# Attention probabilities: from TensorE transposes to DMA transposes of 16-bit halves, with the row sums divided out of the weighted heads

## What is computed

```python
x = x + xattn(ctx, layernorm(x), ...)      # 64 sequences, 16 heads of 64
# in xattn, with ln1/ln2 the learned layer norms:
xn, ln = layernorm(ctx, ln1), layernorm(layernorm(x), ln2)
q = ln @ Wq
k, v = split(concat([xn, ln], axis=-2) @ Wkv)        # 256 keys per sequence
w = softmax(q k^T / 8)                                # [head, 128 tokens, 256 keys]
out = (w @ v) @ Wo
```

## Time and profile before

| | us |
|---|---|
| median of 3 runs (lowest to highest) | 3361.94 (3360.63 to 3364.99) |
| span of the profiled execution, first to last instruction | 3360.9 |
| attention: start to its first score matmul | 28.39 |
| first score of round 0 to first score of round 127 | 1789.31 |
| from there to the last add of the attention | 26.4 |
| the other stages | the rest, about 1516 |

### The profile page before, as it was taken

How to read it: one execution, slowest core, us unless ns; L and a number is a source line. 1 busy time by engine, 2 the same in 40 slices (tenths; PEclk the granted TensorE clock), 3 DMA queues, 4 the chain that set the end, 5 groups by cost and what they waited for, 6 DMA issues and landing times. The chain is left out here.

```text
span 3360.9 us, 63900 instructions
## 1 busy us (share of the span) xinstructions
PE 3093.8 (92%) x23118; PEld 2678.5 (80%) x23118; DVE 2444.6 (73%) x5419; ACT 1759.1 (52%) x4520; POOL 1306.3 (39%) x1215
## 2 busy tenths in 40 slices
PE   7999999999999999999999999999999973168987
PEld 6888888888888888888888788888888861046665
DVE  6666666666666666666666787878787848889997
ACT  5555656565656565656564333333333325259997
POOL 2333333333333333333333333333333320048987
PEclk9999999999999999999999999999999985579999
DMA  4000000000000000000001212121212125001111
GB/s 160 5 8 5 8 5 8 5 8 4 8 5 8 4 8 5 8 4 8 5 5 48 64 45 71 45 71 45 70 45 71 45 62 80 0 27 45 45 39 38
DMA packets 108790, 103.92 MB, mean 31 GB/s; under 512 B 26584, under 2 KB 87744, under 8 KB 108480
## 3 DMA queue, kind: packets, MB, share of 16 engines
q1 hardware_dynamic: 108480, 99.84, 10.3%
HBM read 86.61 MB, written 13.21 MB: 30 GB/s over the span
## 5 line engine op out<-in xcount | busy, mean ns | idle before, releaser
L794 POOL TENSOR_TENSOR attention_prob<-attention_prob,attention_inv_sums 128x1024 f32<-128x1024 f32 x256 | 479.6, 1895 | 400.1 <-DVE attention_inv_sums L652 400.1
L504 ACT ACTIVATE attention_prob<-attention_turns,attention_neg_max 128x256 f32<-128x256 f32 x1024 | 468.5, 482 | 175.2 <-DVE attention_neg_max L643 175.2
L1371 POOL TENSOR_TENSOR experts_hidden_lo<-experts_weighed,experts_hidden_hi 128x512 fp32r<-128x512 f32 x192 | 255.0, 1328 | 531.4 <-ACT experts_hidden_hi L1124 531.4
L659 DVE COPY attention_probT<-attention_turns 128x512 f32<-128x512 f32 x512 | 329.0, 684 | 163.0 <-PE attention_turns L380 162.9
L346 PE MATMUL attention_turns<-kv_hi,wkv 128*128 128x512 f32 x1024 | 374.2, 406 | 0.6 <-DVE wkv L622 0.6
L643 DVE TENSOR_REDUCE attention_neg_max<-attention_turns 128x2 f32<-128x512 f32 x512 | 318.1, 684 | 45.1 <-PE attention_turns L370 44.3
L1124 ACT ACTIVATE experts_hidden_hi<-experts_weighed 128x512 fp32r<-128x512 f32 x192 | 121.4, 632 | 403.8 <-DVE experts_weighed L1261 403.8
L314 PE MATMUL attention_turns<-wkv,kv_hi 128*128 128x512 f32 x1024 | 329.1, 403 | 2.1 <-DVE kv_lo L677 2.1
L495 ACT COPY attention_v<-attention_turns 128x512 f32<-128x512 f32 x256 | 150.1, 586 | 309.8 <-PE attention_turns L314 309.8
L380 PEld LDWEIGHTS attention_turns<-ident,attention_prob 128*128 128x128 f32 x2048 | 240.0, 141 | 36.6 <-POOL attention_prob L794 3.3
L380 PE MATMUL attention_turns<-ident,attention_prob 128*128 128x128 f32 x2048 | 265.9, 273 | 2.8 <-POOL attention_prob L794 2.8
(11 more groups left out here) (296 smaller groups left out, 8939.1 us busy)
## 6 DMA issues: line engine op xcount, KB each, us to landing
experts_spread<-shares SPq DMA_DIRECT2D x256, 128.0 KB, 3.0
attention_ctx<-in_ctx SPq DMA_DIRECT2D x32, 256.0 KB, 2.7
experts_far_ctxT<-in_ctxT SPq DMA_DIRECT2D x32, 256.0 KB, 3.5
weights_ctx<-in_ctx SPq DMA_DIRECT2D x16, 512.0 KB, 3.9
out<-conv_x_out SPq DMA_DIRECT2D x15, 512.0 KB, 2.8
x_all<-in_x SPq DMA_DIRECT2D x7, 1024.0 KB, 9.0
first_x<-norms SPq DMA_DIRECT2D x16, 256.0 KB, 3.2
dist<-experts_far SPq DMA_DIRECT2D x16, 256.0 KB, 2.5
```

The source lines that it names most:

```text
L504: made = act.activation(prob[n % 2][:, h, :], bank_of("s", 2 * n + e)[:, m * 256:(m + 1) * 256], ACT.Exp, bias=neg_max[:, n % 2, 2 * e + m ...
L659: dve.tensor_copy(probT[n % 2][:, 2 * g:2 * g + 2].rearrange("p h t c -> p (h t c)"), bank_of("t", 2 * n + g)[:, :]).then_inc(p_copied, 1)
L794: pool.tensor_tensor(prob[n % 2][:, :, :], prob[n % 2][:, :, :], inv[:, n % 2, :].unsqueeze(2).broadcast_to([P, QH, 2 * TOK]), ALU.mult).t ...
L1371: pool.tensor_tensor(hid_lo[n % 3][:, :], weighed[n % 2], hid_hi[n % 3][:, :].bitcast(F32), ALU.subtract).then_inc(hid_split, 1)
```

## The change

Transposing and normalising the probabilities change hands:

- ACT's exponentials signal after every two heads instead of four. GpSimd no longer multiplies; `split(n)` copies each half unit (two heads, 512 float32 words seen as 1024 16-bit halves) into two planes, low halves and high halves (`planes`), by one copy of 128x1024 16-bit elements. Two such copies per unit.
- SP issues a DMA transpose per half unit (`turn_planes`), 128x1024 16-bit elements, from `planes` into `planesT`. `planesT` has one place per half unit, so a transpose waits until the unit before has been joined.
- GpSimd's `join(n)` copies the transposed planes back into 32-bit words (`probT`), again two copies of 128x1024 16-bit elements per unit. TensorE's `turn_probs` and DVE's `copy_probs` are gone.
- The values are weighted with the raw exponentials. DVE multiplies the weighted heads in PSUM by the inverse sums (`scale_heads`), in columns that SP has written to DRAM (`store_inverses`, one DMA per round) and loaded back, broadcast over partitions (`load_inverses`, two DMAs per round), into `attT_lo`, whose old content the output projection must have read.
- `weigh_values(w)` runs two rounds after its scores instead of one (`LAG` = 2), and each round makes its own share of the output (12 matmuls), summed over four rounds in a bank of its own (`out_ps`). `add_out` is once per pair.
- The projections of the values move from the round before into their own round, and the value weights are loaded last of the three. In `inputs` the parts of the layer norms are cut finer and spread over other places. The loads of `following` come behind the last `load_inverses`, and the semaphores of the staged weights are shared by both stages.

The core of the diff:

```diff
...
+    LAG = 2
...
+        planes = [st.sb(f"planes{i}", [P, 2, 2, QH * TOK], U16) for i in range(2)]
+        planesT = st.sb("planesT", [P, 2, 2, QH * TOK], U16)
...
-        heads_out = st.bank("heads_out")
+        out_ps = st.bank("out")
...
-        for src, dst, c in ((wkv, wkv_p, INNER), (wq, wq_p, 0), (wkv, wkv_p, 0)):
+        for src, dst, c in ((wq, wq_p, 0), (wkv, wkv_p, 0), (wkv, wkv_p, INNER)):
...
+            def turn_planes(n, g):
+                sp.wait_ge(planes_made, 2 * n + g + 1)
+                if n:
+                    sp.wait_ge(joined, 2 * n + g - 1)
+                sp.dma_start_transpose(planesT[:, g, :, :].rearrange("p b (c l) -> p (b c) l", l=TOK),
+                                       planes[n % 2][:, g, :, :].rearrange("p b c -> p (b c)")
+                                       ).then_inc(p_turned[g], 16)
+
+            def store_inverses(u):
+                sp.wait_ge(inverted, 2 * u + 2)
+                if u >= 2:
+                    sp.wait_ge(inv_loaded, 32 * (u - 1))
+                sp.dma_start(inv_rows[u % 2].rearrange("o t c -> t o c"),
+                             inv[:, u % 2, :, :, :].rearrange("p o e m -> p o (e m)")).then_inc(inv_stored, 16)
+
+            def load_inverses(w):
+                sp.wait_ge(inv_stored, 16 * (w + 1))
+                if w:
+                    sp.wait_ge(out_made, w)
+                for o in range(2):
+                    sp.dma_start(inv_cols[o * HEAD:(o + 1) * HEAD, :],
+                                 inv_rows[w % 2, o:o + 1].rearrange("o t c -> o (t c)").broadcast_to([HEAD, 4 * TOK])
+                                 ).then_inc(inv_loaded, 16)
...
+            for u in range(ROUNDS + LAG):
+                p, i = divmod(u, QUADS)
+                if u >= LAG:
+                    load_inverses(u - LAG)
+                if 0 < u <= ROUNDS:
+                    for g in range(2):
+                        turn_planes(2 * u - 1, g)
+                if u < ROUNDS:
+                    if i == 3 and p + 2 < PAIRS:
+                        load_ctx(p + 2)
+                    store_inverses(u)
+                    for g in range(2):
+                        turn_planes(2 * u, g)
+                if not u:
+                    sp.wait_ge(w_split, WO)
+                    for n in range(FREE_LOADS, len(X_LOADS)):
+                        load_x(n)
...
+            for u in range(ROUNDS + LAG):
                 n = 2 * u
-                more = u + 1 < ROUNDS
                 if u < ROUNDS:
                     score(n)
                     score(n + 1)
-                if u:
-                    weigh_values(u - 1)
...
+                if u >= LAG:
+                    weigh_values(u - LAG)
+                if u + 1 < ROUNDS:
+                    project_k(n + 2)
+                    project_q(u + 1)
+                    project_k(n + 3)
+                if u < ROUNDS:
+                    project_v(n)
+                    project_v(n + 1)
+                if u >= LAG:
+                    output(u - LAG)
...
+            def scale_heads(w):
+                dve.wait_ge(weighed, w + 1)
+                dve.wait_ge(inv_loaded, 32 * (w + 1))
+                bank = bank_of("w", w)[:, :].rearrange("p (c t) -> p c t", c=4)
+                dve.tensor_tensor(bank, bank, inv_cols.rearrange("p (t c) -> p c t", c=4), ALU.mult).then_inc(scaled, 1)
...
+            def split(n):
+                for g in range(2):
+                    pool.wait_ge(exped, 2 * n + g + 1)
+                    words = prob[n % 2][:, 2 * g:2 * g + 2, :].rearrange("p h c -> p (h c)").bitcast(U16)
+                    pool.tensor_copy(planes[n % 2][:, g, :, :], words.rearrange("p (c b) -> p b c", b=2)
+                                     ).then_inc(planes_made, 1)
+
+            def join(n):
+                if n >= 2:
+                    pool.wait_ge(weighed, n // 2)
+                for g in range(2):
+                    pool.wait_ge(p_turned[g], 16 * (n + 1))
+                    words = probT[n % 2][:, 2 * g:2 * g + 2, :, :].rearrange("p h t c -> p (h t c)").bitcast(U16)
+                    pool.tensor_copy(words.rearrange("p (c b) -> p b c", b=2), planesT[:, g, :, :]).then_inc(joined, 1)
...
+            for u in range(ROUNDS + 1):
+                n = 2 * u
                 p, i = divmod(u, QUADS)
...
+                for j in range(2):
+                    if u:
+                        join(n - 2 + j)
+                    if u < ROUNDS:
+                        split(n + j)
```

More of the change, by code:

```diff
@@ L430, in pe_program @@
                 project_k(c)
-            for u in range(ROUNDS + 1):
+            for u in range(ROUNDS + LAG):
                 n = 2 * u
-                more = u + 1 < ROUNDS
                 if u < ROUNDS:
@@ L716, in dve_program @@
                 low_k(c)
-            for u in range(ROUNDS + 1):
+            low_weight(4)
+            low_weight(5)
+            for u in range(ROUNDS + LAG + 1):
                 n = 2 * u
                 p, i = divmod(u, QUADS)
-                more = u + 1 < ROUNDS
-                norm_next = p + 1 < PAIRS and not i
+                measured = 1 if not u else p + 2 if i == 3 and p + 2 < PAIRS else None
+                following_pair = p + 1 if p + 1 < PAIRS else None
                 if u < ROUNDS:
```

340 lines of the change are left out of this document (160 added, 180 removed).

## The result

The changed kernel takes 3254.86 us (median of 4 runs, 3252.75 to 3256.71) against 3363.06 for the kernel before, measured beside it (4 runs, 3360.63 to 3364.99): a ratio of 0.9678, 95% interval 0.9665 to 0.9692. That is 108 us faster, where 195 were forecast.

What follows compares the result with a forecast made beforehand. TensorE's own work was taken to bound the rounds, at 14.09 us each. 3361.9 - 207 for the transposes leaving + 12 at the edges gave 3167 us; likeliest case 3141 to 3195 (chance 0.53), wide range 3140 to 3600.

Steps and rivals of the forecast that it cites:

- TensorE's saving: Attention rounds: 16 transposes leave TensorE, 1.63 us a round, 14.09 to 12.46, saving 207 us over 127 rounds.
- I cost both at nothing; cover is some 2.5 us: Attention round: later high parts on ScalarE (0.6 us) and the output's wait for its low part cost nothing.
- `scale_heads` 0.7, inverse sums at 3.8: VectorE's added pass takes about 0.7 us; the inverse sums it waits for land near 3.8 us into the round.
- 1.13: GpSimd: price c in us of each of eight added copies per round, making GpSimd 10.3 us of 12.46.
- the turning point of 1.40: GpSimd: copy price c, in us, up to which TensorE stays the bound.
- My estimate of 1.54: GpSimd: copy price in us from the skill's 1.8 cycles per element, 13.6 us a round; the trace disagreed.
- Transposes: DMA transpose per half unit: 3.6 to 3.8 us from issue to landing, where up to 4.9 is allowed.
- my third rival: Ring of join, transpose, join slower than before, deciding from a landing time of 5.7 us; 3553 us at 6.4; chance 0.17.
- The edges: Before and after the rounds: 2 us gained at the start, 8 lost at the first weighting, 6 in the tail; +12.
- rival 1: GpSimd sets the pace below the old one, copies 1.40 to 1.59 or transposes 4.9 to 5.7 us: 3195 to 3355; chance 0.14.
- signs of being wrong: Copies above 1.4 us, `join` idle for transposes, `scale_heads` waiting with ScalarE behind it, first weighting long after 60, tail over 35.
- the signs of the forecast: Mid-kernel: clock 1.00, TensorE over 98% busy, rounds 12.4 to 12.6 us, copies near 1.1, transposes under 4.9.

Runs made afterwards that it cites:

- experiment 1: Changed kernel with SP issuing the context's load first in every fourth round, ahead of inverse-sum loads and transposes: 3172.6 us, ratio 0.9438 to the kernel before.
- experiment 2: Changed kernel with SP's order kept and VectorE's measuring of the context moved to the end of the round: 3175.36 us, ratio 0.9446 to the kernel before.
- experiment 5: On experiment 1, VectorE's normalisation of the context moved behind the second low part of the keys: 3157.24 us, ratio 0.9392 to the kernel before.
- experiment 7: On experiment 5, `scale_heads` reads the inverse sums one after another instead of every fourth, so against wrong columns: 3152.83 us, ratio 0.9383 to the kernel before.
- experiment 4: On experiment 1, each GpSimd join preceded by an added copy of a quarter of its elements: 3232.93 us, ratio 0.9611 to the kernel before.
- experiment 8: Four kernels on experiment 5: x loads a round later, 3155.22 us; tail reordered, 3156.86; both, 3156.63; x loads later plus next weights early from ScalarE's queue, 3159.11.
- experiment 3: On experiment 1, no loads of inverse sums, `scale_heads` multiplying by a tile of weights: 3145.51 us, ratio 0.9356 to the kernel before.

## Why the prediction was right or wrong

**TensorE's saving: right, a little small.** I took 1.63 us a round. Undisturbed pairs take 49.13 against 56.27 (14.07 x 4), so 1.79. My start-to-start reading stopped at the next instruction: the pair of matmuls behind the first piece of transposes took 0.71 us, where the same pair takes 0.62 now. That is 0.09, and the second piece had 0.87, not 0.84; the last 0.04 I can't place. On 127 rounds it is 230 us from 14.09 to 12.28, not 207.

**"I cost both at nothing; cover is some 2.5 us": the step that failed.** The cover was there for the work that I listed. I listed one round and left out what only one round in four does: in i = 3 the context's measurement, in i = 0 two normalisations. The wait for the inverse sums I did see, and that it would eat this cover. I also asked which transposes stand behind what in SP's queue, but not what stands behind the transposes: `load_ctx`, in the diff, two lines below them. The price: 84.5 us for the late context, of which 29.8 is longer busy time of TensorE and not waiting (experiments 1 and 2), and 15 for `norm_ctx` ahead of `k_lo` while the inverse sums are late (experiment 5). Some 10 more remain in experiment 5: rounds 0 to 2, and rounds i = 1 with 12.75.

**`scale_heads` 0.7, inverse sums at 3.8.** `scale_heads` was 1.09, for the stride (experiment 7); the sums let it start 4.8 us into the round shown of the changed kernel and 5.9 into the one of experiment 1.

**GpSimd: right within its bounds.** 1.13 was forecast; `split` has 1.06, `join` 1.37, the mean is 1.21, under the turning point of 1.40; experiment 4, past it by the sum, lost 0.46 us a round. My estimate of 1.54, worked out from the Trainium skill's 1.8 cycles (GPSIMD Engine Reference, 3.1), is above both. (What is left without the multiplication is 5.00 - 3.79 = 1.21 us, not 1.25, which changes nothing.) What I missed is that GpSimd can be hidden for TensorE and still slow VectorE.

**Transposes: right side.** 3.2 us, forecast 3.6 to 3.8; the bound is 4.9, and `join` waited 71.6 us for them in 512 copies. The Trainium skill's 1309 ns for a block (VectorE: DVE Perf Modes, The three transpose paths; not a page on DMA, as my third rival has it) would have made eight blocks 10.5 us; the whole transpose took 3.2.

**The edges: sum too small, and the parts wrong.** The first weighting came at 54.70, not near 61; rounds 0 to 2 took 39.6 us, 2.6 more than three undisturbed ones, where I had 8, and the x loads were not their cause. (Round 0 is short, 9.62, without weighting and output; rounds 1 and 2 have 13.53 and 16.48, and why is open.) The tail lost 16.3, not 6. In it the heads of round 127 wait in VectorE's order behind the splits of weights that SP loads behind the last inverse sums, but undoing that order shortened nothing (experiment 8). What the sums themselves cost there is 5.7 (experiment 3); the rest is not placed.

**The sum.** -230 + 84.5 + 15 + 10 - 0.8 + 16.3 - 1.1 = -106.1, against -105.9 measured. It closes because its terms are differences of the same spans; what the experiments show are the 84.5 and the 15. The measured time, 3255, lies inside my wide range (3140 to 3600) but outside the forecast (3141 to 3195), and that the wide range holds it is luck: it was drawn so wide for GpSimd and the transposes. It lies in the band of rival 1, but for another reason: neither GpSimd nor the ring of transposes set the pace. (The 3584 for c = 1.8 counts the 12 us twice; by my own sum it is 3572.) Two of my signs of being wrong did come: `scale_heads` waiting for the inverse sums with ScalarE behind it (123.4 and 18.4 us in the rounds), and a tail over 35 us. The clock of 1.00 and over 98% busy that I named as the signs of the forecast were absent in the changed kernel, and present in experiment 5 (1558.40 of 1569.59 us, 99.3%), which with 3157 us is inside the forecast's own range.

## What to carry over

When work leaves the engine that sets the pace, list what every engine and queue does in each kind of round, also in the rounds that occur once in four, and follow each queue to what stands behind the moved instruction, not only to what stands ahead of it. A DMA whose data are needed once in a while goes first in the queue, and a wait for it goes last on the engine that others wait for. An engine with slack can still cost time, by the instructions of another engine that it holds up.

## What the runs showed of the hardware

- A GpSimd copy of 1024 16-bit elements takes 1.06 us when it reads every second element (`split`) and 1.37 when it writes to every second place (`join`).
- The DMA's transpose of 128 x 1024 16-bit elements lands after 3.2 us; with 3 MB of loads under way two of them hold SP's queue 7.3 us instead of 2.6.
- VectorE's `tensor_scalar` of 256 fp32 elements in SBUF, 0.41 us, takes up to 1.57 beside GpSimd's copies, with a median of 1.12; its `k_lo`, which reads PSUM, kept its 0.68.
- A read of every fourth fp32 element in SBUF makes a VectorE multiplication of 512 elements 1.09 us instead of 0.70.
- With one wait of 1.7 to 2.8 us in about 52 us TensorE's clock fell to 1.2 GHz behind 13 of 30 such waits; its mean went from 1.00 to 0.98, and its matmuls were busy 29.8 us more over 127 rounds, of which the clock accounts for at most 23.9.
